# The FFN's low part on VectorE in one operation, the normalisations on GpSimd

## What is computed

```python
x = x + tanh(g_xattn[0]) * attention(layernorm(x), ctx, ctx)        # causal, 16 heads
n = layernorm(x)
prob = softmax(n @ w_router + b_router)
mask = top 4 of the 16 blocks, for each token
h = relu(einsum('nd,ebd->neb', n, w1b) + b1b)
y = einsum('neb,ebd,ne->nd', h, w2b, mask) + b2
x = x + tanh(g_ffn[0]) * y
```

## Time and profile before

| | |
|---|---|
| median of the runs | 695.56 us |
| span of the profiled execution | 694.6 us |
| TensorE busy | 671.8 us, 97% |
| VectorE busy | 519.7 us, 75% |
| ScalarE busy | 511.9 us, 74% |
| GpSimd busy | 564.2 us, 81% |

### The profile page before, as it was taken

One profiled execution on the slowest core, in us unless ns is written; L12 is line 12 of the kernel. 1 busy time (PEld: TensorE's weight loads), 2 busy tenths in 40 slices (PEclk: granted clock), 3 DMA queues, 4 the chain that ended last, 5 costly groups with the idle time before them and its releaser, 6 DMA issues.

```text
span 694.6 us, 30557 instructions
## 1 busy us (share of the span) xinstructions
PE 671.8 (97%) x13072; PEld 623.5 (90%) x13072; DVE 519.7 (75%) x1429; ACT 511.9 (74%) x785; POOL 564.2 (81%) x778
## 2 busy tenths in 40 slices
PE   6779999999999999999999999999999999999998
PEld 5668899999999999999989999999999999999997
DVE  6788877877777787787787787778777777877752
ACT  3657787787787878778778777877877877786642
POOL 5687889889888888988988988898898888886642
PEclk9989999999999999999999999999999999999999
DMA  5322345444335354344444444533533544342010
GB/s 162 95 78 39 83 114 75 106 113 80 95 101 110 86 99 113 79 82 113 113 79 103 105 72 99 114 95 86 113 83 82 110 113 77 75 83 50 20 38 32
DMA packets 161814, 61.90 MB, mean 89 GB/s; under 512 B 135696, under 2 KB 161424, under 8 KB 161680
## 3 DMA queue, kind: packets, MB, share of 16 engines
q1 hardware_dynamic: 160848, 58.38, 37.7%
q10 hardware_dynamic: 832, 1.57, 0.8%
HBM read 19.03 MB, written 8.39 MB: 39 GB/s over the span
## 4 chain that ended last, share of the span: by engine, by line
PE 87%; DVE 4%; POOL 3%; SPq 2%; DMA 1%; issue 1%; ACT 1%; POOLq 0%; DVEq 0%
PE bank L411 10%; PE score_banks L332 10%; PE score_banks L302 8%; PE bank L413 8%; PE bank L412 8%; PE bank L436 8%; PE bank L435 8%; PE bank L434 8%; PE bank L345 8%; PE bank L359 4%; PE bank L370 3%; PE bank L381 1%; PE score_banks L315 1%; DMA qT<-qT 1%; PE bank L389 1%
## 5 line engine op out<-in xcount | busy, mean ns | idle before, releaser
L837 POOL TENSOR_TENSOR h_low<-hid,h_high 128x512 fp32r<-128x512 f32 x128 | 164.8, 1287 | 12.8 <-ACT hid L535 12.6
L709 DVE SCALAR_TENSOR_TENSOR hid<-bank,b_cols,used_all 128x256 f32<-128x256 f32 x248 | 108.2, 478 | 73.0 <-PE bank L413 66.9
L513 ACT ACTIVATE weights<-score_banks 128x1024 f32<-128x1024 f32 x128 | 124.3, 1023 | 40.3 <-PE score_banks L332 40.3
L411 PE MATMUL bank<-xT_high,w_high 128*128 128x256 f32 x496 | 150.7, 304 | 0.3 <-DVE hid L709 0.2
L830 POOL TENSOR_SCALAR_AFFINE_SELECT weights<-weights 128x1024 f32<-128x1024 f32 x128 | 138.3, 1105 | 8.6 <-ACT weights L513 8.2
L413 PE MATMUL bank<-xT_high,w_low 128*128 128x256 f32 x496 | 139.2, 281 | 0.0
L412 PE MATMUL bank<-xT_low,w_high 128*128 128x256 f32 x496 | 139.1, 280 | 0.0
L434 PE MATMUL bank<-w_high,h_high 128*128 128x256 f32 x488 | 137.3, 281 | 0.7 <-POOL h_low L837 0.7
L436 PE MATMUL bank<-w_high,h_low 128*128 128x256 f32 x488 | 138.0, 283 | 0.0
L435 PE MATMUL bank<-w_low,h_high 128*128 128x256 f32 x488 | 137.5, 282 | 0.0
L794 POOL TENSOR_SCALAR ve<-mv 128x1 f32<-128x1 f32 x128 | 34.6, 271 | 89.9 <-DVE mv L620 89.8
(11 more groups left out here) (102 smaller groups left out, 1508.4 us busy)
## 6 DMA issues: line engine op xcount, KB each, us to landing
x_in<-in_x SPq DMA_DIRECT2D x31, 256.0 KB, 3.3
out_y<-y_out SPq DMA_DIRECT2D x31, 256.0 KB, 2.4
c_in<-in_ctx SPq DMA_DIRECT2D x30, 256.0 KB
qT<-qT SPq DMA_DIRECT2D x128, 4.0 KB
w_stage<-in_w1T ACTq DMA_DIRECT2D x1, 1024.0 KB, 5.9
hid<-in_w2T SPq DMA_DIRECT2D x8, 128.0 KB, 2.7
kT_parts<-k_parts SPq DMA_TRANSPOSE x57, 2.8
qT_parts<-q_parts SPq DMA_TRANSPOSE x57, 2.7
```

The source lines that it names most:

```text
L411: pe.matmul(out=bank, lhsT=w1_high[:, k, c], rhs=high, start=k == 0, stop=False)
L513: act.activation(weights[:, b % 2, half * 2 * HB:(half + 1) * 2 * HB, :].rearrange("p h q -> p (h q)"), score_banks[:, 2 * half:2 * half + ...
L709: dve.scalar_tensor_tensor(hid[:, n % 4, j], hid_bank(n)[:, j * TOKS:(j + 1) * TOKS], b1_cols[:, c:c + 1], used_all[:, p % 2], ALU.add, AL ...
L837: pool.tensor_tensor(h_low[:, p % 2, chunks], hid[:, n % 4], h_high[:, p % 2, chunks].bitcast(F32), ALU.subtract).then_inc(h_low_made, 1)
```

## The change

hidden_low moves from GpSimd to VectorE. It becomes one operation, max(hid, 0) minus h_high, on the unclipped hid, so ScalarE's clipping in place goes. On VectorE it stands twice in an iteration: for the second piece of the iteration before after row_maximum, ahead of hidden_masked(m); and for the first piece after route, ahead of hidden_masked(m+1). normalised and normalised_again move from VectorE to GpSimd, behind the rstd of tile i-2 and, for normalised, behind x2_b2. Waits are added where an engine had been its own guard: layernorm_stats waits for qn_made, attention_added for xn_made and x2_b2_made, row_maximum for q_turned or q_parts_made, normalised_again for x_turned.

```diff
                 act.wait_ge(hid_made, HC * p + PC * (m + 1))
-                act.activation(h_high[:, p % 2, chunks], hid[:, n % 4], ACT.Relu)
-                act.activation(hid[:, n % 4], hid[:, n % 4], ACT.Relu).then_inc(hid_clipped, 1)
+                act.activation(h_high[:, p % 2, chunks], hid[:, n % 4], ACT.Relu).then_inc(h_high_made, 1)
...
+                if b >= 2:
+                    dve.wait_ge(qn_made, b - 1)
                 stats_of(x_in[:, b % XS, :], stats1, mv1, b % 2, b, x_stats, x_mean)
...
                 carrier = b + MAX_LAG
-                if carrier >= N:
+                if carrier - QS >= QUERIES_BY_PE:
                     dve.wait_ge(q_parts_made, carrier - QS - QUERIES_BY_PE + 1)
+                elif carrier >= QS:
+                    dve.wait_ge(q_turned, carrier - QS + 1)
...
+                elif b >= 2:
+                    dve.wait_ge(xn_made, b - 1)
+                    dve.wait_ge(x2_b2_made, b - 1)
                 dve.scalar_tensor_tensor(x2[:, s], att[:], tanh_g[:, 0:1], x_in[:, b % XS, :],
                                          ALU.mult, ALU.add).then_inc(x2_made, 1)
...
+            def hidden_low(p, m):
+                n = PIECES * p + m
+                chunks = slice(PC * m, PC * (m + 1))
+                dve.wait_ge(h_high_made, n + 1)
+                dve.scalar_tensor_tensor(h_low[:, p % 2, chunks], hid[:, n % 4], 0.0,
+                                         h_high[:, p % 2, chunks].bitcast(F32), ALU.max, ALU.subtract
+                                         ).then_inc(h_low_made, 1)
...
                     attention_added(i - 2)
-                if 0 <= i + 3 < N:
-                    normalised(i + 3)
                 if 0 <= i + 1 < N:
                     row_maximum(i + 1)
-
-                early = q_early(i)
-                if early and 0 <= i - 2 < N:
-                    normalised_again(i - 2)
+                if last_p is not None:
+                    hidden_low(last_p, last_m + 1)
                 if p is not None:
                     hidden_masked(p, m)
                 weights_low(i)
-                if not early and 0 <= i - 2 < N:
-                    normalised_again(i - 2)
...
                     route(pr)
+                if p is not None:
+                    hidden_low(p, m)
...
+            def normalised_again(b):
+                s = b % 2
+                pool.wait_ge(rstd2_made, b + 1)
+                if b >= 2:
+                    pool.wait_ge(x_turned, b - 1)
+                pool.tensor_scalar(xn[:, s], x2[:, s], mv2[:, s, 0:1], rstd2[:, s],
+                                  ALU.subtract, ALU.mult).then_inc(xn_made, 1)
...
                     rstd_of(mv2, ve2, rstd2, b % 2, b, x2_mean, ve2_made, rstd2_made)
+                    normalised_again(b)
...
                     pool.tensor_tensor(x2_b2[:, b % GS, :], x2[:, b % 2], gated_b2[:], ALU.add).then_inc(x2_b2_made, 1)
-                last_p, last_m = hidden_pair(i - 1)
-                if last_p is not None:
-                    hidden_low(last_p, last_m + 1)
+                if 0 <= i + 3 < N:
+                    if i + 3 == 0:
+                        pool.wait_ge(q_levels_set, LEVELS)
+                    normalised(i + 3)
                 if QUERIES_BY_PE <= i + 3 < N + MAX_LAG:
                     query_parts(i + 3)
...
                     causal_weights(i)
-                if p is not None:
-                    hidden_low(p, m)
                 weights_low(i)
```

More of the change, by code:

```diff
@@ L167, in build @@
         att_copied, x_copied, xT_high_made = sem("att_copied"), sem("x_copied"), sem("xT_high_made")
-        hid_clipped, w_high_made = sem("hid_clipped"), sem("w_high_made")
+        h_high_made, w_high_made = sem("h_high_made"), sem("w_high_made")
         route_copied, used_made, tanh_done = (sem(n) for n in ("route_copied", "used_made", "tanh_done"))
@@ L667, in attention_added @@
                 stats_of(x2[:, s], stats2, mv2, s, b, x2_stats, x2_mean)
[L669 to L673, removed]
             def x_parts(b):
@@ L747, in _ @@
                 p, m = hidden_pair(i)
+                last_p, last_m = hidden_pair(i - 1)
                 if 0 <= i - OUT_LAG - 1 < N:
@@ L796, in rstd_of, with normalised @@
                 pool.tensor_tensor(result[:, s], ve[:, s], half_power[:], ALU.pow).then_inc(rstd_made, 1)
+            def normalised(b):
+                s = b % 2
+                pool.wait_ge(rstd1_made, b + 1)
+                if QUERIES_BY_PE <= b - QS:
+                    pool.wait_ge(q_parts_made, b - QS - QUERIES_BY_PE + 1)
+                elif b >= QS:
+                    pool.wait_ge(q_turned, b - QS + 1)
+                pool.tensor_scalar(q_pad[:, b % QS, :, 0:HD], x_in[:, b % XS, :].rearrange("p (h d) -> p h d", d=HD),
+                                  mv1[:, s, 0:1], rstd1[:, s], ALU.subtract, ALU.mult).then_inc(qn_made, 1)
+            def normalised_again(b):
+                s = b % 2
+                pool.wait_ge(rstd2_made, b + 1)
[3 more added lines that the diff above has]
+                                  ALU.subtract, ALU.mult).then_inc(xn_made, 1)
             def values(b):
@@ L831, in causal_weights @@
                                        pattern=[[0, 2 * HB], [1, S]], channel_multiplier=-1).then_inc(weighted, 1)
-            def hidden_low(p, m):
-                n = PIECES * p + m
-                chunks = slice(PC * m, PC * (m + 1))
-                pool.wait_ge(hid_clipped, n + 1)
-                pool.tensor_tensor(h_low[:, p % 2, chunks], hid[:, n % 4], h_high[:, p % 2, chunks].bitcast(F32),
-                                   ALU.subtract).then_inc(h_low_made, 1)
             def weights_low(i):
```

## The result

The changed kernel takes 739.07 us (median of four runs, 735.06 to 740.46), the kernel before 695.66 beside it: a ratio of 1.061, 95% interval 1.0587 to 1.0634. It is 43 us slower. The profiled execution has a span of 736.6 us against 694.6.

What follows compares the result with a forecast made beforehand. TensorE was taken as the bound, at 20.43 us a pair. Span 694.6 + 2 (collision) + 3.5 (queries' chain) - 2.5 (fill) - 0.7 (end) = 696.9 us, as a time 697.9; range 691.5 to 705.

Steps and rivals of the forecast that it cites:

- The bound: Steady part: TensorE busy 553.5 of 554.0 us, 20.43 us a pair; savings elsewhere worth nothing unless TensorE waits for them.
- GpSimd's price: Each normalisation as tensor_scalar on GpSimd: taken as 0.45 us, upper end 0.74; 58 us for 128, at most 95.
- The queries' chain: q_parts through SP's transpose and riding maximum to shifted_scores: 14 slow transposes overrun by 0.25 us, +3.5 us (0 to 10).
- The place on VectorE: Second hidden_masked and VectorE's queue behind it wait for ScalarE's h_high; finished begins 0.8 us later in a light iteration.
- the +2 of the prediction: Steady part: a third of the 54 iterations overruns TensorE's slack by 0.1 us, +2 us (0 to 11).
- the path of the prediction: Delayed second low part makes hidden_masked(m) end at about 11.1 us, leaving TensorE's hidden(m+1) 0.25 to 0.35 us of slack.
- the end: Last iterations: the last h_low takes 0.75 us on VectorE instead of 1287 ns, the Relu ahead of it goes: -0.7 us.
- The collision: VectorE's two-input low parts and GpSimd block each other: the second meets x2_b2, the first affine_select; +2 us.
- The fill: Before the steady part: normalisations and their rstd waits leave VectorE's queue, q_transposed waits 1.2 us less: -2.5 us (-4 to 0).
- The third: Rival: GpSimd's tensor_scalar costs 0.74 us, each steady iteration overruns through the collision, 11 us in all: 707 us, chance 0.12.

Runs made afterwards that it cites:

- low_behind: Kernel before with only the low part moved to VectorE, both low parts placed behind what TensorE waits for: 695.19 us, ratio 0.9991.
- early_q: Changed kernel with only GpSimd's order changed: normalised first in the iteration, x2_b2 behind q_parts: 709.39 us, ratio 1.0181.
- early_q_late: early_q with the first piece's low part moved behind hidden_masked(m+1) on VectorE: 702.23 us, ratio 1.0102.
- low_xearly: Low part on VectorE, normalisations also on VectorE; against the half without GpSimd, normalised_again moved right behind row_maximum: 713.41 us, ratio 1.0226.
- the half without GpSimd: Changed kernel with both normalisations back on VectorE in their old places, the low part still on VectorE: 712.42 us, ratio 1.0236.
- x_dve: Changed kernel with normalised_again back on VectorE in its old place, normalised still on GpSimd: 718.72 us, ratio 1.0315.
- early_q_fill: early_q with the normalisations of tiles 0 to 8 on VectorE: 700.91 us, ratio 1.0072.
- sp_order: Changed kernel with the riding maximum's DMA put ahead of the transpose of used in SP's queue: 734.98 us, ratio 1.0528.

## Why the prediction was wrong

**The bound** was right: TensorE's 20.43 us a pair, where a saving elsewhere is worth nothing. low_behind, with 65 us less busy time on ScalarE and 138 less on GpSimd, shows it.

**GpSimd's price** is the step that failed. The prediction bounded its tensor_scalar by the copy (0.40 us) and the two-input operation (0.74), and took 0.45 because both read one tensor. The operation takes 1.24 us, half a microsecond above the upper end and three times the 0.41 us that the prediction gave as an estimate beside its own figure. What it reads is not what it costs: 0.93 us with one operation, 1.11 with two constants. No row of the kernel before showed arithmetic with a scalar on a wide tile on GpSimd; its only such row, L794, is one element wide. The bound was drawn through rows of another kind of operation, and the upper end should have stood well above both.

**The queries' chain** was named with its stations in the right order, and sized at 3.5 us. It was 28.5. The first mistake is the price again. The delay of q_parts was put at 0.9 us; with the measured price it is 0.9 + 2 times 0.8 = 2.5, and the timelines show the queries' transpose 2.3 us later in a router iteration. The second is where the slack was looked for. The prediction took it as used up only where SP's transposes were slow, 14 times; but in a router iteration SP's own queue passes the delay on, 24 times in 27. Before, the riding maximum was issued there 4.2 us ahead of the next L332, after it is 3.0, and that is late: a slack of 1.2 us at most. By an estimate from these figures the 0.9 us of the prediction would have fitted into it, and 2.3 us are 1.1 too many, which is what a pair has lost (28.5 us in 27 pairs). So with the price right and the slack asked for in each pair, the trace of the kernel before would have given a loss of this size.

**The place on VectorE** was right as a mechanism and hidden by the larger loss. In the changed kernel hidden(m+1) is not late on the mean (S + 1.30 and 1.52, as before), since the other stall gives VectorE time. In early_q, where that stall is gone, the wait for h_high costs 3.0 us of the steady part (early_q_late takes it away), near the +2 of the prediction, but not by its path: hidden(m+1) isn't late there, and TensorE's waits are again those for the small DMA. By the path of the prediction, hidden(m+1), it costs time in low_xearly, where VectorE has the normalisations too. What was missed is normalised_again in the half without GpSimd, 0.5 us a pair, a place the change itself doesn't have, and the end: the prediction gave 0.7 us back there, the wait for h_high takes 1.9, and only with the low part moved the end is 0.5 us shorter than before.

**The collision** is half right. One of the changed kernel:

```profile
435.33 2.60 POOL L843 TENSOR_SCALAR_AFFINE_SELECT weights<-weights 128x1024 f32<-128x1024 f32 x2
...
435.82 1.16 DVE L707 SCALAR_TENSOR_TENSOR h_low<-hid,h_high 128x512 fp32r<-128x512 f32 x1 [2.12 <-ACT h_high L534]
```

The 26 low parts that began after an affine_select half took 0.79 to 1.64 us, and 17 that began ahead of one took 0.69. The prediction counted this side alone (its sum of GpSimd's work ahead of affine_select, 3.05 us, comes to 3.07, which changes nothing). The other side is that 38 affine_select halves that began behind a low part took 1.16 to 1.62 us instead of 1.10: together 14 us more on GpSimd. The second low part, expected to be held up by x2_b2, mostly met GpSimd's normalisation, and 57 times took 0.7 us beside it, not held up. It began 0.4 us or more after the normalisation, mostly 0.6. Where it began 0.2 to 0.3 us after it (six cases in other runs) it took 0.85 to 0.89. And where the low part was under way when the normalisation began, the normalisation took longer: 1.77 us in x_dve (0.02 us behind it), 1.67 in early_q_late (0.5 to 1.0 behind). So this pair does collide, at the start of the normalisation. The rule of the Trainium skill (SBUF — State Buffer, section "Who interferes with whom"), that the two engines exclude each other and the order of issue decides which one is blocked, holds here for affine_select (the numbers above); for the normalisation it holds at its start and not for the whole instruction. The row that the prediction took as agreeing (1.42 us against 0.48) doesn't show the order: there VectorE's operation had begun 0.04 us ahead of the affine_select and was held up all the same.

**The fill** was forecast 2.5 us shorter and became 8.6 longer. The gain at its head, 1.2 us for q_transposed, didn't come: that L271 waited 1.48 us for GpSimd's q_pad instead of 2.29 for VectorE's, but started at 13.28 us instead of 12.63. In the four kernels with all normalisations on VectorE tile 8 starts at 85.5 to 87.5 us, around the 86.4 of the kernel before, so no gain of 2.5 us shows there either. The granted clock of the fill fell too (0.94 to 0.85); it costs little by itself, since early_q_fill has 0.90 up to tile 8 and starts it at 86.4.

**The rivals.** The third named the right culprit (GpSimd's tensor_scalar dearer than taken), still at too low a price, and through the wrong door: hidden_masked instead of q_parts. Its 707 us is far below 739, and the range ended at 705. At the measured price its own arithmetic, 0.2 us over at 0.6 us of delay, would give 1.2 us over at 1.6 us, 65 us in 54 iterations; the loss of 43 us would lie below that, so the arithmetic would not have been right either.

## What to carry to other kernels

A step that moves to another engine is paid by what stands behind it in that engine's queue, and by every queue after that: follow the hand-over through the DMA issuer to the instruction that waits, and count the issues in between. Where the trace has no row of the same arithmetic on that engine, the neighbours' durations are no upper bound; ask at which price the chain breaks, and whether that price can be excluded. And when an engine gets new work with slack in its total, put it behind what the bound waits for: here the same work cost 16.5 us in one place and nothing in another.

## What the runs showed of the hardware

- GpSimd's tensor_scalar on 128x256 fp32 took 1.24 us with two operations and both scalars in SBUF, 1.11 with two constants, 0.93 with one operation and its scalar in SBUF, beside 0.40 for a copy and 0.74 for a two-input addition.
- Neither that instruction nor a two-input VectorE operation on 128x512 was slowed where the latter began 0.4 us or more behind the former (57 times 0.7 us, beside a median of 1.242, in the changed kernel); where the latter began 0.02 us ahead, the tensor_scalar took 1.77 us (51 times in x_dve). affine_select did hold it up (up to 1.64 us), and was held up itself where it began second (up to 1.62 us instead of 1.10).
- One-input copies do hold up a low part, or are held up by it: beside q_parts in low_xearly the low part took 1.24 us instead of 0.68, or the copy 1.40 instead of 0.75.
- The granted clock fell to 0.50 for some 3 us behind four of the idle times of TensorE in sp_order (1.9 to 2.5 us long), and not behind two others of 1.6 and 2.1 us. At that level an L332 stage took 2.09 us (tile 0 of the changed kernel, tile 4 of the kernel before) where it takes 1.17 at the full clock.
